# Where VectorE counts slot positions and gates, and where Pool scatters them, beside the latent maxima of a fused attention and expert kernel

## The chip, the cores and the metric

The kernel runs on one core of a Trainium2 chip. What counts is the device time of one execution, in microseconds: the median of three runs is 956.13 (955.96 to 956.14).

## What is computed

Eight batches of 256 tokens with 256 features are normalised. One branch is latent attention (MLA: low-rank queries, keys and values, a rotary part of 64, 16 heads, causal). The other is a transformer block: plain causal attention (MHA, 16 heads), a residual, and a mixture of eight experts of which each token takes two. The output is x + s * silu(f), with s and f the results of the branches. Cut to what bears on the change:

```python
def _moe(x_flat, Wr, Wg, Wu, Wd):
    logits = x_flat @ Wr.T
    top_logits, top_idx = jax.lax.top_k(logits, TOP_K)      # TOP_K = 2, 8 experts
    probs = jax.nn.softmax(top_logits, axis=-1)
    cw = jnp.zeros((T, NUM_EXPERTS), x_flat.dtype)
    cw = cw.at[jnp.arange(T)[:, None], top_idx].add(probs)
    hg = jnp.einsum('eih,th->eti', Wg, x_flat)
    hu = jnp.einsum('eih,th->eti', Wu, x_flat)
    y = jnp.einsum('ehi,eti->eth', Wd, jax.nn.silu(hg) * hu)
    return jnp.einsum('eth,te->th', y, cw)
```

## The kernel before

Each engine has one hand-written queue of instructions; semaphores order them between engines, and nothing reorders them. The attention part is a pipeline over the eight batches b. In each batch TensorE runs four stages: P2 (heads of MHA transposed), T1 (MLA scores of batch b, their exponentials, values, and beside them the MHA scores from which the row maxima are taken), P1 (MLA projections of batch b+1) and T2 (MHA scores of batch b, exponentials and values, and beside them the MLA scores of batch b+1 for their row maxima).

T2 is where the change lies. For each of 16 heads TensorE issues the transposed MHA scores of head h, then the MLA scores of head h-1 of the next batch (`max_head`, into one of two PSUM banks). ACT takes the exponential of head h into `ex`, Pool sets the part above the diagonal to zero (`causal`, an affine_select per head), and for each group of four heads TensorE multiplies by the values (`values`, which waits for the selects of its four heads). VectorE takes the maxima of the MLA scores (`maxima`, two instructions and two reads of an accumulator for each head); TensorE's `max_head(h)` waits for the maxima of head h-2, for its bank. Ahead of the maxima of every second head VectorE rounds two heads of queries (`rounded`, the cast of `qr`), which TensorE waits for too. Behind head 5 TensorE runs `project_v2`, which overwrites the bank ps[1] with the rank counts and so waits for `pst` (the second step of the positions), and behind head 10 `project_qk2`. Both are projections of MHA for the next batch. The stage ends at line L602, where TensorE transposes the row maxima (`max_t`); then P2 starts with transposes that ACT and VectorE (`odd_heads`, the cast of `qt`) move to SBUF.

The routing of batch r = b-1 runs beside this. VectorE finds the top two experts (`top_two`), TensorE counts ranks (`route_ranks`, five small bf16 matmuls in T2 behind head 1), VectorE works out slot positions (`positions`: nine small instructions, most of which wait for one just before) behind the maxima of head 1 and gates (`gates`: four) behind head 4. Pool scatters 4 x 128 slot entries to a list in DRAM by four indirect DMAs (`scatter_slot`), one behind each of the selects of heads 9 to 12. Batch 0's T2 has no routing to do; the T2 of batch 7 has no next batch, so it has no MLA maxima, no projections, and its positions and gates run in one piece; VectorE and ACT split expert weights there instead. After the last T2 the last batch's routing runs alone, and once its slots are scattered the experts' blocks start.

Three functions of VectorE make up what the hooks `after` hold, as `after[h]` runs behind the maxima of head h; `splits` has hooks behind 3, 5, 7, 12 and 14.

## Time and profile before

| | us |
|---|---|
| median of three runs | 956.13 |
| the profiled execution, its time | 958.59 |
| its span, first to last instruction | 956.9 |
| mean granted TensorE clock, share of full | 0.935 |
| TensorE busy | 830.5 (87%) |
| VectorE busy | 625.2 (65%) |
| ACT busy | 501.6 (52%) |
| Pool busy | 392.2 (41%) |

The profile is one execution taken by the hardware profiler. PE is TensorE (PEld its weight loads), DVE VectorE, ACT ScalarE, POOL GpSimd. A line such as L586 is a line of the kernel; helpers that issue many operations have one line for all of them. In brackets stands how long an engine sat idle ahead of an instruction, and which engine's result ended that. The attention part runs to about 652 us; the experts' blocks fill the rest.

### The profile page before, as it was taken

What the parts mean: (1) busy time and instruction counts of PE and PEld (TensorE: products, weight loads), DVE (VectorE), ACT (ScalarE), POOL (GpSimd) and SP (SyncE); (2) the same over time, 40 slices, a digit from 0 to 9 for tenths busy, and PEclk for the clock granted to TensorE, in tenths of its full rate; (3) what the DMA queues carried; (4) which work ended last, traced back from release to release, by engine and by line L of the source; (5) the groups of instructions that cost most, each with busy time, mean ns of one, the idle gap of its engine ahead of it and who ended that gap; (6) DMA issues with size and microseconds to landing.
All of it is one profiled execution on the core that took longest, in us unless ns stands there. A gap on an engine that the chain in (4) does not pass through costs nothing.

```text
span 956.9 us, 18123 instructions
## 1 busy us (share of the span) xinstructions
PE 830.5 (87%) x6432; PEld 743.6 (78%) x6432; DVE 625.2 (65%) x2207; ACT 501.6 (52%) x1089; POOL 392.2 (41%) x538
## 2 busy tenths in 40 slices
PE   5889999999999999999998998965269999998980
PEld 3868978978887887887897897843169999998980
DVE  4876677667677667757758757632257777776754
ACT  3445375366366456456356446540146677776651
POOL 5522432343343334344344344331404756555541
PEclk9878999999999999999999999976579999999995
DMA  8000000000000000000000000030236776889736
GB/s 273 1 1 2 13 1 25 12 2 13 24 1 14 13 13 2 24 12 3 23 13 2 24 12 3 23 144 23 47 134 176 221 220 198 238 240 348 193 53 186
DMA packets 39884, 71.04 MB, mean 74 GB/s; under 512 B 10914, under 2 KB 34850, under 8 KB 36834
## 3 DMA queue, kind: packets, MB, share of 16 engines
q1 hardware_dynamic: 29074, 57.39, 17.6%
q0 software_dynamic: 9856, 12.13, 6.7%
q8 instruction: 52, 0.85, 0.4%
q10 hardware_dynamic: 864, 0.36, 0.2%
q14 instruction: 38, 0.31, 0.1%
HBM read 55.12 MB, written 14.81 MB: 73 GB/s over the span
## 4 chain that ended last, share of the span: by engine, by line
PE 67%; DVE 10%; DMA 9%; issue 6%; POOL 2%; ACT 2%; SPq 2%; POOLq 0%; DVEq 0%; ACTq 0%
PE ps L586 54%; DMA expert_rows<-yo,slot_of 6%; PE ps L679 6%; PE ps L716 3%; DVE ps L1400 2%; PE ps L612 2%; DVE ps L1397 1%; SPq L425 1%; PE ps L621 1%; DVE qr L1237 1%; DMA w_ukv_raw<-in_w_ukv 1%; DMA raw<-in_w_experts 1%; SPq L441 1%; POOL slots L515 1%; POOL expert_rows L563 1%
## 5 line engine op out<-in xcount | busy, mean ns | idle before, releaser
L523 POOL TENSOR_SCALAR_AFFINE_SELECT ex<-ex 128x256 f32<-128x256 f32 x256 | 107.6, 425 | 246.5 <-ACT ex L1101 245.1
L1101 ACT ACTIVATE ex<-ps 128x384 f32<-128x384 f32 x256 | 125.4, 497 | 118.9 <-PE ps L586 116.8
L586 PE MATMUL ps<-qt,kt 128*128 128x256 f32 (+1 forms) x768 | 164.1, 325 | 8.6 <-ACT ex L1101 4.6
L502 POOL TENSOR_TENSOR tok<-tok,swp 128x256 f32<-128x256 f32 x128 | 97.4, 761 | 114.7 <-DVE swp L1362 113.7
L1397 DVE CUSTOM_DVE_ANT_0 ps<-ps,mask 128x128 f32<-128x128 f32 x256 | 77.4, 302 | 94.9 <-PE ps L586 90.5
L586 PEld LDWEIGHTS ps<-qt,kt 128*128 128x128 f32 x768 | 108.9, 193 | 20.7 <-issue 9.8
L563 POOL DMA_INDIRECT expert_rows<-yo,slot_of x46 | 78.5, 1707 | 110.8 <-DMA expert_rows<-yo,slot_of 55.6
L1400 DVE CUSTOM_DVE_ANT_0 ps<-ps,mask 128x256 f32<-128x256 f32 x256 | 118.9, 465 | 0.0
L1241 DVE TENSOR_TENSOR wel<-raw,weh 128x768 fp32r<-128x768 f32 x92 | 88.4, 961 | 37.2 <-ACT weh L971 36.0
L586 PE MATMUL ps<-wh,xth 128*128 128x320 f32 (+2 forms) x352 | 96.9, 358 | 3.7 <-DVE wl L1241 2.8
L1358 DVE TENSOR_TENSOR tok<-ps,cos_t 128x320 f32<-128x320 f32 x128 | 62.9, 491 | 52.8 <-PE ps L586 52.2
L586 PE MATMUL ps<-xeh,weh 128*128 128x256 f32 x368 | 79.4, 298 | 11.8 <-issue 9.9
L971 ACT ACTIVATE qt<-ps 128x512 f32<-128x512 f32 (+1 forms) x96 | 57.2, 596 | 61.9 <-PE ps L679 59.8
L971 ACT ACTIVATE kt<-ps 128x512 f32<-128x512 f32 (+1 forms) x96 | 57.4, 598 | 53.4 <-PE ps L679 48.3
L586 PE MATMUL ps<-wh,xtl 128*128 128x320 f32 (+2 forms) x352 | 84.1, 321 | 0.0
L586 PE MATMUL ps<-wl,xth 128*128 128x320 f32 (+2 forms) x352 | 83.8, 320 | 0.0
L971 ACT ACTIVATE weh<-raw 128x768 fp32r<-128x768 f32 x92 | 77.9, 846 | 10.1 <-DMA raw<-in_w_experts 10.1
L679 PE MATMUL ps<-idf,tok 128*128 128x128 f32 x512 | 77.0, 273 | 0.0
L586 PE MATMUL ps<-xeh,wel 128*128 128x256 f32 x368 | 75.9, 289 | 0.0
L586 PE MATMUL ps<-xel,weh 128*128 128x256 f32 x368 | 75.8, 288 | 0.0
L586 PE MATMUL ps<-kt,qt 128*128 128x128 f32 (+1 forms) x256 | 73.4, 368 | 0.0
L586 PE MATMUL ps<-kr,qr 128*128 128x128 f32 (+1 forms) x256 | 58.6, 316 | 16.8 <-DVE negm L1400 13.1
(160 smaller groups left out, 1918.3 us busy)
## 6 DMA issues: line engine op xcount, KB each, us to landing
raw<-in_w_experts SPq DMA_DIRECT2D x23, 1536.0 KB
mla_branch<-s_b SPq DMA_DIRECT2D x8, 256.0 KB, 2.1
expert_rows<-xn SPq DMA_DIRECT2D x8, 256.0 KB, 2.2
x_normalised<-otk SPq DMA_DIRECT2D x8, 256.0 KB, 2.1
xr<-in_x SPq DMA_DIRECT2D x1, 2048.0 KB
s_tok<-mla_branch SPq DMA_DIRECT2D x1, 2048.0 KB
w_cols_raw<-in_w_cols SPq DMA_DIRECT2D x1, 1792.0 KB, 15.4
x<-expert_rows SPq DMA_DIRECT2D x3, 512.0 KB, 5.2
```

The costliest lines, as they stand in the source:

```text
L502: nc.gpsimd.tensor_tensor(t, t, swp[:, n % 2, :, :], ALU.add).then_inc(tokd, 1)
L523: nc.gpsimd.affine_select(a, a, [[0, 2], [1, P]], ALU.is_ge, zero, 0, -1).then_inc(exm, 1)
L563: nc.gpsimd.indirect_dma_start(ys[:, :], bass.IndirectOffsetOnAxis(mt_b[:, blk, j, 1:2], 0), yo[:, blk % 2, j, :], None, compute_op=ALU.ad ...
L586: return nc.tensor.matmul(o, a, m, start=start, stop=stop, skip_group_check=True, **k)
L679: t = nc.tensor.transpose(ps[2 + n % 2][:, j * P:(j + 1) * P], tok[:, n % 4, j, :], idf[:, :])
L716: i = nc.tensor.transpose(bank2(u)[:, j * P:(j + 1) * P], a[:, p0:p0 + P], idf[:, :])
L971: return nc.scalar.activation(o, a, ACT.Copy)
L1101: nc.scalar.activation(ex[:, h % (2 * G), :], ps[4 + h % 2][:, P:4 * P], ACT.Exp, scale=scale).then_inc(ex_, 1)
L1241: return nc.vector.tensor_tensor(o, a, b.bitcast(F32), ALU.subtract)
L1358: nc.vector.tensor_tensor(tok[:, n % 4, :, 0:HW], a, cos_t[:, tt:tt + 1, :].broadcast_to([P, G, HW]), ALU.mult)
L1397: nc.vector.tensor_tensor_reduce(out=o[:, 0:P], in0=o[:, 0:P], in1=mask2[:, 1, :], scale=-1.0, scalar=-2.0 * BIG, op0=ALU.add, op1=ALU.min ...
L1400: nc.vector.tensor_tensor_reduce(out=o[:, S:2 * S], in0=o[:, S:2 * S], in1=mask2[:, :, :].rearrange("p a k -> p (a k)"), scale=-1.0, scala ...
```

## The change

VectorE's `positions` is divided into five steps and `gates` into three. In the T2 stages of batches 1 to 6 they are no longer two pieces behind the maxima of heads 1 and 4; they go behind the maxima of heads 1, 2, 4, 6, 8 (two steps), 9 and 10. The instructions, their operands and the semaphores that they wait for and raise are as before. Where they run alone (the T2 of batch 7 and behind it) they still follow each other at once. Pool's four scatters of a batch no longer stand between the selects of heads 9 to 13; they stand behind the select of head 15, with one wait for `posd` ahead of the first. This goes for batches 1 to 7.

```diff
@@ block.gpsimd
-            def scatter_slot(r, t, k):
-                if t == 0 and k == 0:
-                    pool.wait_ge(posd, r + 1)
-                nc.gpsimd.indirect_dma_start(slot[:, :], bass.IndirectOffsetOnAxis(posu[:, t, k:k + 1], 0),
-                                             meta[:, t, k, :], None).then_inc(msc, 16)
+            def scatter_slots(r):
+                pool.wait_ge(posd, r + 1)
+                for t in range(2):
+                    for k in range(2):
+                        nc.gpsimd.indirect_dma_start(slot[:, :], bass.IndirectOffsetOnAxis(posu[:, t, k:k + 1], 0),
+                                                     meta[:, t, k, :], None).then_inc(msc, 16)
...
-            def slots_between(r):
-                return {9 + 2 * t + k: lambda t=t, k=k: scatter_slot(r, t, k) for t in range(2) for k in range(2)}
...
                 rope_sums(b + 1)
-                causal(b, ex2, exm2, slots_between(b - 1))
+                causal(b, ex2, exm2, {})
+                scatter_slots(b - 1)
             causal(last, ex1, exm1, {6: lambda: power2(last - 1)})
-            causal(last, ex2, exm2, slots_between(last - 1))
+            causal(last, ex2, exm2, {})
+            scatter_slots(last - 1)
             power2(last)
-            for t in range(2):
-                for k in range(2):
-                    scatter_slot(last, t, k)
+            scatter_slots(last)
@@ block.vector
                     if not first:
-                        after[1] = lambda: positions(b - 1)
-                        after[4] = lambda: gates(b - 1)
+                        in_expert, chosen, summed, kept, stepped = position_steps(b - 1)
+                        plus_one, inverse, both = gate_steps(b - 1)
+                        after |= {1: in_expert, 2: chosen, 4: summed, 6: kept, 8: lambda: (stepped(), plus_one()),
+                                  9: inverse, 10: both}
                     stage_m1(b + 1, after)
...
             def positions(r):
-
-                dve.wait_ge(rnk, r + 1)
...
+                for step in position_steps(r):
+                    step()
 
             def gates(r):
-
-                dve.wait_ge(gex, r + 1)
...
+                for step in gate_steps(r):
+                    step()
```

The steps hold what `positions` and `gates` held, in the same order: `in_expert` pose; `chosen` base and two of posx; `summed` posf; `kept` posu and two of meta (with the wait for the scatters of the batch before); `stepped` rc; `plus_one` and `inverse` gsum; `both` two of meta, which raises `posd`.

## Rows read from the trace of the kernel before

**Rows 1.** The page, the chain that ended last, by engine.

```profile
PE 67%; DVE 10%; DMA 9%; issue 6%; POOL 2%; ACT 2%; SPq 2%; POOLq 0%; DVEq 0%; ACTq 0%
```

**Rows 2.** Timeline of PE at L602: start, us, engine, line, operands, count [idle before <-releaser].

```profile
143.04 0.38 PE L602 MATMUL ps<-idf,negm 128*16 128x128 f32 x2 [0.54 <-DVE negm L1400]
...
219.64 0.39 PE L602 MATMUL ps<-idf,negm 128*16 128x128 f32 x2 [0.34 <-DVE negm L1400]
...
370.21 0.39 PE L602 MATMUL ps<-idf,negm 128*16 128x128 f32 x2 [0.34 <-DVE negm L1400]
...
444.72 0.39 PE L602 MATMUL ps<-idf,negm 128*16 128x128 f32 x2 [0.34 <-DVE negm L1400]
...
595.57 0.39 PE L602 MATMUL ps<-idf,negm 128*16 128x128 f32 x2 [0.34 <-DVE negm L1400]
```

**Rows 3.** Timeline of PE: latent scores of head 0 in batches 0 and 4, head 4.

```profile
126.08 0.49 PE L586 MATMUL ps<-kr,qr 128*128 128x128 f32 x2 [0.21 <-ACT kt L971]
...
425.92 0.50 PE L586 MATMUL ps<-kr,qr 128*128 128x128 f32 x2 [0.21 <-ACT kt L971]
...
430.31 0.47 PE L586 MATMUL ps<-kr,qr 128*128 128x128 f32 x2 [1.12 <-DVE negm L1400]
```

**Rows 4.** Timeline of DVE in T2 of batch 4.

```profile
427.79 0.17 DVE L1521 TENSOR_TENSOR pose<-ps,base 128x16 f32<-128x16 f32 x1
428.00 0.17 DVE L1524 TENSOR_TENSOR base<-ps,base 128x8 f32<-128x8 f32 x1
428.08 0.25 DVE L1526 TENSOR_TENSOR posx<-oh,pose 128x16 f32<-128x16 f32 x2
...
429.10 0.41 DVE L1237 CAST qr<-qt 128x512 fp32r<-128x512 f32 x1
...
431.99 0.16 DVE L1547 TENSOR_SCALAR gsum<-gexp 128x2 f32<-128x2 f32 x1
...
432.66 0.30 DVE L1397 CUSTOM_DVE_ANT_0 ps<-ps,mask 128x128 f32<-128x128 f32 x1
...
440.17 0.76 DVE L1237 CAST qr<-qt 128x512 fp32r<-128x512 f32 x1
```

**Rows 5.** Line L1237 on DVE, 199 to 620 us: ns min/median/max, starts.

```profile
L1237 DVE CAST qr<-qt x46: 412/420/824, 202.1 to 591.0; 128x512 fp32r<-128x512 f32 x46
```

**Rows 6.** Stretches: us, PE busy (x), granted clock, DMA share, GB/s.

```profile
126.00:129.00 3.00, 2.57 (x15) 1.00 0.00 0
...
204.00:206.00 2.00, 2.00 (x12) 0.50 0.00 0
...
580.00:582.00 2.00, 2.00 (x11) 0.50 0.03 8
...
648.00:650.00 2.00, 0.12 (x4) 0.50 0.02 1
```

**Rows 7.** Timelines of ACT, POOL and PE at the end of batch 7's T2.

```profile
645.06 0.93 ACT L1101 ACTIVATE ex<-ps 128x384 f32<-128x384 f32 x2
...
648.69 1.13 POOL L523 TENSOR_SCALAR_AFFINE_SELECT ex<-ex 128x256 f32<-128x256 f32 x3
...
649.88 0.65 PE L586 MATMUL ps<-ex,v 128*32 128x256 f32 x4 [3.02 <-POOL ex L523]
```

**Rows 8.** Timeline of DVE, T2 of batch 0: maxima of heads 5, 10 and 11.

```profile
131.52 0.30 DVE L1397 CUSTOM_DVE_ANT_0 ps<-ps,mask 128x128 f32<-128x128 f32 x1 [0.53 <-PE ps L586]
...
136.76 0.30 DVE L1397 CUSTOM_DVE_ANT_0 ps<-ps,mask 128x128 f32<-128x128 f32 x1 [0.32 <-PE ps L586]
...
138.22 0.30 DVE L1397 CUSTOM_DVE_ANT_0 ps<-ps,mask 128x128 f32<-128x128 f32 x1 [0.71 <-PE ps L586]
```

**Rows 9.** Line L515 on POOL, the scatters: ns min/median/max, starts.

```profile
L515 POOL DMA_INDIRECT slots<-meta,posu x32: 957/977/1220, 211.2 to 675.8; - x32
```

**Rows 10.** Timeline of POOL: first select of batch 7, a scatter behind another.

```profile
601.87 0.41 POOL L523 TENSOR_SCALAR_AFFINE_SELECT ex<-ex 128x256 f32<-128x256 f32 x1 [7.54 <-ACT ex L1101]
...
673.25 0.96 POOL L515 DMA_INDIRECT slots<-meta,posu  x1 [0.30 <-issue]
```

More of the change, by code:

```diff
@@ L1543, in gates, with position_steps, in_expert, chosen @@
-            def gates(r):
-                dve.wait_ge(gex, r + 1)
-                g = meta[:, :, :, 2].bitcast(F32)
-                nc.vector.tensor_scalar(gsum[:, :], gexp[:, :], 1.0, None, ALU.add).then_inc(gst, 1)
-                dve.wait_ge(gst, 3 * r + 2)
-                nc.vector.reciprocal(gsum[:, :], gsum[:, :]).then_inc(gst, 1)
-                dve.wait_ge(gst, 3 * r + 3)
-                copy(g[:, :, 0], gsum[:, :])
-                nc.vector.tensor_tensor(g[:, :, 1], gexp[:, :], gsum[:, :], ALU.mult).then_inc(posd, 1)
+            def position_steps(r):
+                def in_expert():
+                    dve.wait_ge(rnk, r + 1)
+                    nc.vector.tensor_tensor(pose[:, :, :], ps[1][:, 0:2 * NE].rearrange("p (t e) -> p t e", t=2),
+                                            base[:, :].unsqueeze(1).broadcast_to([P, 2, NE]), ALU.add).then_inc(pst, 1)
+                def chosen():
+                    dve.wait_ge(pst, 6 * r + 2)
+                    nc.vector.tensor_tensor(base[:, :], ps[1][:, 2 * NE:3 * NE], base[:, :], ALU.add).then_inc(pst, 1)
+                    for t in range(2):
+                        i = nc.vector.tensor_tensor(posx[:, t, :, :], oh[:, t, :, :],
+                                                    pose[:, t:t + 1, :].broadcast_to([P, 2, NE]), ALU.mult)
+                    i.then_inc(pst, 1)
+                def summed():
+                    dve.wait_ge(pst, 6 * r + 4)
+                    nc.vector.tensor_reduce(posf[:, :, :].rearrange("p t k -> p (t k)"),
+                                            posx[:, :, :, :].rearrange("p t k e -> p (t k) e"), AX.X,
+                                            ALU.add).then_inc(pst, 1)
+                def kept():
+                    dve.wait_ge(pst, 6 * r + 5)
+                    wait(dve, msc, 64 * r)
+                    copy(posu[:, :, :], posf[:, :, :])
+                    ids = rc[:, C_IDS:C_IDS + 8].rearrange("p (t k f) -> p t k f", t=2, k=2)
+                    for t in range(2):
+                        i = copy(meta[:, t, :, 0:2], ids[:, t, :, :])
+                    i.then_inc(pst, 1)
+                def stepped():
+                    dve.wait_ge(pst, 6 * r + 6)
+                    step = rc[:, C_IDS:C_IDS + 8].rearrange("p (a f) -> p a f", f=2)
+                    nc.vector.tensor_scalar(step[:, :, :], step[:, :, :], 2.0 * P, None, ALU.add).then_inc(gst, 1)
+                return in_expert, chosen, summed, kept, stepped
@@ new lines, in gate_steps, with plus_one, inverse, both @@
+            def gate_steps(r):
+                g = meta[:, :, :, 2].bitcast(F32)
+                def plus_one():
+                    dve.wait_ge(gex, r + 1)
+                    nc.vector.tensor_scalar(gsum[:, :], gexp[:, :], 1.0, None, ALU.add).then_inc(gst, 1)
+                def inverse():
+                    dve.wait_ge(gst, 3 * r + 2)
+                    nc.vector.reciprocal(gsum[:, :], gsum[:, :]).then_inc(gst, 1)
+                def both():
+                    dve.wait_ge(gst, 3 * r + 3)
+                    copy(g[:, :, 0], gsum[:, :])
+                    nc.vector.tensor_tensor(g[:, :, 1], gexp[:, :], gsum[:, :], ALU.mult).then_inc(posd, 1)
+                return plus_one, inverse, both
```

21 lines of the change are left out of this document (removed).

## The prediction, as it was put on record

> **What bounds the kernel now.** I read the chain of work that ended last first: TensorE holds two thirds of it, VectorE a tenth, Pool 2% [rows 1]. So the question is not which engine is busiest but where TensorE waits inside the stages that the change touches. The second view is the timeline of TensorE at line L602, which moves a batch's row maxima for the latent branch and so closes stage T2. From that of batch 0 to that of batch 6 there are six periods in 452.53 us [rows 2], the first and the last line of it. The period of batch 4 is 444.72 - 370.21 = 74.51, that of batch 1 is 219.64 - 143.04 = 76.60. T2 itself runs from the score matmul of the first latent head to L602: 425.92 to 444.72 = 18.80 in batch 4 [rows 2, 3], so the other stages of a period take 74.51 - 18.80 = 55.71. I take that as the same in each batch; the six T2 stages with positions then sum to 452.53 - 6 x 55.71 = 118.3, of which batch 1 has 20.9.
>
> Batch 0 is the comparison that the kernel carries itself. Its T2 has no positions, no gates and no scatters, and takes 143.04 - 126.08 = **16.96** [rows 2, 3]. Batch 4 takes 1.84 more. What lies between shows in three places. (a) TensorE stands 1.12 before head 4's latent scores at 430.31, released by negm, which VectorE writes in its maxima [rows 3]. In that time VectorE ran the positions: 427.79 to 429.10 = 1.31, in one piece between maxima 1 and 2 [rows 4]. (b) The gates, 431.99 to 432.66 = 0.67 [rows 4], cost nothing now: TensorE runs the projection project_v2 just then, and head 5's scores would not be there earlier. (c) The cast of qr at 440.17 takes 0.76 [rows 4], against a median of 0.42 of 46 such casts [rows 5]; a scatter of Pool runs beside it.
>
> A third view, the stretches with their granted clock, adds a cost that the busy times hide. [...]
>
> Last, the T2 of batch 7. It has no latent maxima beside it, so Pool is what ends last. ACT ends the last two exponentials at 645.06 + 0.93 = 645.99; Pool's selects of heads 13 to 15 start only at 648.69, behind the fourth scatter, and TensorE stands 3.02 for them until 649.88 [rows 7]. All that follows (heads to tokens, output, router, last scatters) hangs on that chain.
>
> **The change, part by part.** *Positions and gates in pieces (six stages, batches 1 to 6).* The same 13 instructions stay. In one piece a dependent one starts 0.21 after the one before (427.79 to 428.00), an independent one 0.08 (428.00 to 428.08) [rows 4]. With maxima between them the results are there long before, so I price each at 0.08: 13 x 0.08 = 1.04 instead of 1.31 + 0.67 = 1.98. Where each lands, against the slack that VectorE has in batch 0:
> - behind maxima 1, pose: 0.08 to 0.21, ahead of maxima 2, which TensorE's wait (a) hangs on. Counted 0.1.
> - behind 2 and 4: base, two posx (0.24) and the sum (0.08): VectorE waits 0.53 before maxima 5 in batch 0 [rows 8]; covered. If project_v2 were not there, 0.3 would be paid.
> - behind 6: posu and two copies to meta, 0.24 by pitch, up to 0.5 where they meet a select of Pool. Maxima 7 follow at once in the trace, and TensorE's score 9 waits for them. On the path: 0.24.
> - behind 8 and 9: three instructions, 0.24 to 0.4 against 0.32 of slack before maxima 10 [rows 8]: 0 to 0.1, taken 0.05.
> - behind 10: two, 0.16 against 0.71 before maxima 11 [rows 8]: covered by project_qk2 on TensorE.
> - new waits: each is on VectorE's own earlier step, on gex (done at about head 3) or on the scatters of the batch before (70 us old). project_v2 waits for base, which now ends before head 4's scores do: nothing.
> - the rank matmuls, which batch 0 lacks: 0.1 on TensorE.
>
> *Pool's scatters behind select 15.* A scatter takes 0.957 to 1.220, median 0.977, in 32 [rows 9]; back to back one starts about 1.26 after the other (0.96 and 0.30 of issue) [rows 10]. Four are 5.0. In the middle stages they leave the selects of heads 10 to 15 free; that was no bound there (values of the last group follow the maxima), but cast (c) loses its neighbour: its excess of 0.34 goes. In exchange the scatters now lie beside VectorE's last cast of ks: 0 to 0.34, taken about half, 0.15. Queued behind the scatters on Pool are the selects of the next stage: the first of them comes at 601.87 in batch 7 [rows 10], 6.3 behind L602 (595.57 [rows 2]), and Pool's idle before it is 7.54; that is the room for 5.0, with what select 15 comes earlier on top. Behind the scatters of batch 6, in batch 7, stands power2(7), which waits for the chain heads to tokens, output and residual, longer than 5.0: covered.
>
> The new T2 by this: 16.96 + 0.1 + 0.24 + 0.05 + 0.1 + 0.15 = **17.6**. Six of them are 105.6 instead of 118.3: **12.7 less**. This holds a clock that no longer falls, which is 4.7 of the 12.7 (batches 1, 3 and 6 above their equals: 1.7 + 1.5 + 1.5). I take it so because batch 0, with the wait gone, keeps 1.00 throughout.
>
> *The last T2.* Without scatters, select 15 starts at 645.99 + 0.06 and ends 0.41 later: 646.5 instead of 649.8, and the last values start about 646.5 instead of 649.88: **3.4 less**. Bounds: 2.6 if the last two selects meet VectorE's split of expert weights and take twice their 0.4; 5.0 if TensorE's clock, at half from 648 on [rows 6] after the long wait, then stays up for the last values and the transposes behind them.
>
> [...]
>
> **Rivals.**
> 1. *The clock still falls* in about three of six stages. For it: batch 4 has the wait too (1.12 [rows 3]) and no fall, so something else has a part in it. Against: batch 0. It gives 16.1 - 4.7 = 11.4 less: 944.7.
> 2. *VectorE pays every piece.* If slack I call cover is used up (VectorE is the engine whose maxima the scores wait for), T2 is 16.96 + 1.04 + 0.1 + 0.15 = 18.25 and six save 8.8; with 3.4 this is 12.2: 943.9, and with rival 1 948.6.
> 3. *Slower: four scatters stop VectorE at a stage boundary.* Just behind L602 VectorE's casts of qt are links of the chain that opens the next stage, and three or four scatters now fall there. If each of four stops VectorE for its whole 0.98, a period gains 3.9, six 23.5, against 16.1 saved: 963.5. It decides from 16.1 / 6 = 2.7 per period. Against: the casts of qt read PSUM, and VectorE's PSUM maxima keep their length under today's scatters; only SBUF casts stretch.
> 4. *Nothing changes*: 956, if ACT's exponentials, not VectorE, set the pace of the stage. The wait of 3.02 in batch 7 speaks against it alone, and batch 0, where the same exponentials fit into 16.96.
>
> **How the numbers follow.** The sum is made against the profiled execution: span 956.9, its time 958.6, the median of the runs 956.13, so 2.5 lower. I subtract 12.7 + 3.4 = 16.1 from the median: **940.0**; should the timed runs lack one of the three clock falls, it is 1.5 more. Chances: forecast 0.57 (937 to 942.5), rival 1 0.17, rival 2 0.19 (both together within it), rivals 3 and 4 and the unnamed 0.07. Low end: T2 at 17.3 (1.8 more saved) and 5.0 in the last: 936.6. High end: rival 1 or 2 with one more us lost: 946.5. A measurement of this kernel can tell 0.2% (1.9 us) from no change: faster 0.93, same 0.03, slower 0.04.
>
> **What would show it.** In the new trace: periods at L602 near 73.3, all six alike; no wait over 0.3 before score 4; clock 1.00 through T2; casts of qr at 0.42 for head 12; in batch 7 the last values released within 0.7 of the last exponential. Wrong if TensorE's waits for negm move to score 9 with more than 0.5, if VectorE's casts of qt get longer, or if the first select of the next stage waits for nothing but Pool itself.

## The result, and the profile after

| | before | after |
|---|---|---|
| median, us | 956.13 (955.96 to 958.5) | 934.21 (932.99 to 935.59) |
| ratio | | 0.9766, 95% interval 0.9743 to 0.9788 |
| profiled execution, its time | 958.59 | 935.21 |
| its span | 956.9 | 933.3 |
| mean granted TensorE clock | 0.935 | 0.948 |

The change saves 21.9 us, 2.3%. The forecast was 940.0, so 16.1 saved, and its range ended at 936.6: the direction was right, the size was not, and the result lies below the range. Which chip these runs had is not on record. In two later sets, on chips 3 and 6, the same kernel had ratios of 0.978 and of 0.991. The second of these is a finding of its own, told under the experiments.

The chain of work that ended last in the kernel after. TensorE's share was 67% [rows 1].

```profile
PE 71%; DMA 8%; DVE 8%; issue 5%; ACT 4%; POOL 2%; SPq 0%; POOLq 0%; ACTq 0%; DVEq 0%
```

The timeline of TensorE at the line that closes T2, now L600 (it answers to [rows 2]; start, us, engine, line, operands, count, in brackets the wait before):

```profile
143.13 0.38 PE L600 MATMUL ps<-idf,negm 128*16 128x128 f32 x2 [0.54 <-DVE negm L1398]
...
216.12 0.39 PE L600 MATMUL ps<-idf,negm 128*16 128x128 f32 x2 [0.45 <-DVE negm L1398]
...
362.86 0.39 PE L600 MATMUL ps<-idf,negm 128*16 128x128 f32 x2 [0.45 <-DVE negm L1398]
...
435.87 0.39 PE L600 MATMUL ps<-idf,negm 128*16 128x128 f32 x2 [0.45 <-DVE negm L1398]
...
581.90 0.39 PE L600 MATMUL ps<-idf,negm 128*16 128x128 f32 x2 [0.45 <-DVE negm L1398]
```

Six periods take 581.90 - 143.13 = 438.77 instead of 452.53: 13.76 less. Batch 4's is 73.01 instead of 74.51, batch 1's 72.99 instead of 76.60; one of the six has 73.74 (0.7 more, between the end of T2 and that of the next T1, in this execution alone), the others 72.99 to 73.02.

TensorE in T2 of batch 4, the latent scores of heads 0 and 4 (they answer to [rows 3]):

```profile
418.56 0.50 PE L584 MATMUL ps<-kr,qr 128*128 128x128 f32 x2 [0.21 <-ACT kt L969]
...
421.92 0.47 PE L584 MATMUL ps<-kr,qr 128*128 128x128 f32 x2
```

The stage takes 435.87 - 418.56 = 17.31 (18.80 before), and head 4's score waits for nothing, where it stood 1.12. VectorE in the same stage (it answers to [rows 4]):

```profile
420.43 0.17 DVE L1522 TENSOR_TENSOR pose<-ps,base 128x16 f32<-128x16 f32 x1
...
426.18 0.16 DVE L1235 CAST posu<-posf 128x4 uint32<-128x4 f32 x1
426.25 0.23 DVE L1235 CAST meta<-rc 128x4 uint32<-128x4 f32 x2
426.39 0.29 DVE L1395 CUSTOM_DVE_ANT_0 ps<-ps,mask 128x128 f32<-128x128 f32 x1
...
430.28 0.17 DVE L1235 COPY meta<-gsum 128x2 f32<-128x2 f32 x1
430.36 0.16 DVE L1568 TENSOR_TENSOR meta<-gexp,gsum 128x2 f32<-128x2 f32 x1
431.14 0.30 DVE L1395 CUSTOM_DVE_ANT_0 ps<-ps,mask 128x128 f32<-128x128 f32 x1 [0.63 <-PE ps L584]
431.74 0.42 DVE L1235 CAST qr<-qt 128x512 fp32r<-128x512 f32 x1
```

The pieces stand between maxima. The one behind head 6 costs 426.39 - 426.18 = 0.21; behind the last piece VectorE still waits 0.63 for TensorE, so those pieces are covered. The cast of head 12's queries is back at 0.42.

The end of batch 7's T2 and what hangs on it (it answers to [rows 7]), and the clock there (stretch, length, TensorE's busy time and instructions, granted clock, DMA share, GB/s; it answers to [rows 6]):

```profile
632.14 1.53 POOL L524 TENSOR_SCALAR_AFFINE_SELECT ex<-ex 128x256 f32<-128x256 f32 x3 [0.48 <-ACT ex L1099]
632.22 0.93 ACT L1099 ACTIVATE ex<-ps 128x384 f32<-128x384 f32 x2
...
633.72 0.86 PE L584 MATMUL ps<-ex,v 128*32 128x256 f32 x16 [0.31 <-POOL ex L524]
...
638.76 1.99 PE L584 MATMUL ps<-wo,otf 128*128 128x256 f32 x8 [0.69 <-ACT otf L969]
```

```profile
204.00:206.00 2.00, 2.00 (x26) 1.00 0.00 0
580.00:582.00 2.00, 1.55 (x31) 1.00 0.05 9
...
634.00:638.00 4.00, 2.25 (x28) 1.00 0.02 1
638.00:642.00 4.00, 2.07 (x9) 1.00 0.04 5
```

The wait for the selects is 0.31 instead of 3.02, and in this execution TensorE's clock stays full to 642. Before, it was at half there and beyond, and the output projection took 3.78. That row stood outside what I had shown; here it is, from the kernel before, with its clock:

```profile
656.91 3.78 PE L586 MATMUL ps<-wo,otf 128*128 128x256 f32 x8 [0.69 <-ACT otf L971]
```

```profile
650.00:654.00 4.00, 3.35 (x24) 0.50 0.00 0
654.00:658.00 4.00, 2.21 (x7) 0.50 0.00 0
```

The 1.99 of the projection does not come with every execution of the changed kernel. In the profile of the second set below, the same stretch of work runs at full clock up to the projection (1.00 from 626 to 638) and at half in it (0.50 from 639 to 642):

```profile
638.03 3.17 PE L584 MATMUL ps<-wo,otf 128*128 128x256 f32 x8 [0.69 <-ACT otf L969]
```

Over all profiles without the long wait for the selects the projection takes 1.99 to 3.78, with it 3.40 to 3.78. What does recur, in the profiles of the second and third set, is the stretch from the last values to the projection's start: 7.04 with the wait, 5.05 without.

**Where the 23.6 us between the two profiled spans went.** Six periods: 13.76. From the max_t of batch 7's T1 to the last values: 2.48 (27.41 to 24.93). From the last values to the output projection's start: 1.99 (649.88 to 656.91 = 7.03; 633.72 to 638.76 = 5.04), and with the projection itself up to the residual 3.77. From there to the first expert matmul 0.3. In the experts 3.4 (267.17 to 263.76), of which more below. The rest, under 0.1, is the start of the first period.

### The profile page after: what moved, and what is told of

The parts are those of the page before. It is cut to its first block, busy times and chain, and to the rows that moved or that the text cites. A ratio compares the mean times of both kernels' runs of the same rounds, so it can differ in the third digit from the quotient of the medians.

```text
span 933.3 us, 18123 instructions
## 1 busy us (share of the span) xinstructions
PE 823.7 (88%) x6432; PEld 738.2 (79%) x6432; DVE 618.8 (66%) x2207; ACT 500.8 (54%) x1089; POOL 390.8 (42%) x538
## 4 chain that ended last, share of the span: by engine, by line
PE 71%; DMA 8%; DVE 8%; issue 5%; ACT 4%; POOL 2%; SPq 0%; POOLq 0%; ACTq 0%; DVEq 0%
PE ps L584 57%; PE ps L677 6%; DMA expert_rows<-yo,slot_of 5%; PE ps L714 3%; DVE ps L1398 2%; PE ps L610 2%; ACT ex L1099 2%; DVE ps L1395 1%; DMA xg<-x_normalised,slot_of 1%; PE ps L909 1%; PE ps L619 1%; DMA w_ukv_raw<-in_w_ukv 1%; DMA raw<-in_w_experts 1%; POOL expert_rows L561 1%; DVE xr L1686 1%
## 5 line engine op out<-in xcount | busy, mean ns | idle before, releaser
L1186 ACT ACTIVATE sg<-ps 128x256 f32<-128x256 f32 x92 | 35.7, 388 | 70.9 <-PE ps L584 70.9
```

The source lines that it names most:

```text
L1186: nc.scalar.activation(sg[:, n % 2, :], ps[n % 3][:, 0:BS], ACT.Silu).then_inc(sgd, 1)
```

## The experiments

Five sets of kernels ran, each with the kernel before beside it on the same chip; ratios are to that. The first set ran on chip 12, the second and the third on chip 3, the fourth on chip 6 and the fifth on chip 5. Two kernels of the first set ran again on chip 3 and are told here with it.

**First set: one part at a time.** The changed kernel with the scatters back between the selects:

```diff
-                causal(b, ex2, exm2, {})
-                scatter_slots(b - 1)
+                causal(b, ex2, exm2, slots_between(b - 1))
```

> VectorE's positions and gates in pieces as in the changed kernel; Pool's four scatters stay between the selects of heads 9 to 13. Theory A (the two edits need each other): posd now comes behind the maxima of head 10, so Pool stands behind select 9 with the selects of heads 10 to 15 queued behind it; four scatters of 1.0 and six selects from there put the last select some 2.5 us behind its place in the changed kernel. T2 of batches 1 to 6 about 19.8 us against 17.3, last T2 as before: near 957 us. Theory B (the edits add up): T2 about 17.6, time near 944.

Measured: 978.24, ratio 1.0182 (1.0131 to 1.0233), slower than the kernel before. Theory A has the mechanism, as the rows below show, but not its price: T2 took 20.2 to 20.9 and not 19.8, and the clock behind it was not counted. I ran it again on another chip, to see whether it was the program's:

> The changed kernel with the scatters of batches 1 to 7 back between selects 9 to 13 (the same program as the first run of this kind, ratio 1.0182 on another chip). Theory A (split in pieces, the position numbers are ready only after head 9, so Pool stands at its first scatter and the selects 12 to 15 queue behind four scatters at the stage's end; it is the program's): periods of 76.6 to 78.5 us again, the clock at half at the end of each T2, ratio 1.014 to 1.022. Theory D (it was that chip's): ratio 0.98 to 1.00.

Measured: 971.97, ratio 1.0187 (1.0162 to 1.0213), periods of 76.55 to 78.52. It is the program's. The timeline of Pool and TensorE at the end of its T2 of batch 4, and the clock there:

```profile
442.60 1.03 POOL L522 DMA_INDIRECT slots<-meta,posu  x1 [2.73 <-DVE meta L1575]
...
448.55 1.12 POOL L533 TENSOR_SCALAR_AFFINE_SELECT ex<-ex 128x256 f32<-128x256 f32 x3
...
449.72 1.51 PE L591 MATMUL ps<-ex,v 128*32 128x256 f32 x16 [2.58 <-POOL ex L533]
```

```profile
450.00:454.00 4.00, 4.00 (x30) 0.50 0.02 4
```

Split in pieces, the gates are ready only behind head 10. Pool, whose first scatter stands behind select 9, waits 2.73 for them with six selects queued behind, and the last values stand 2.58. The granted clock is 0.50 for 3.4 us at the end of T2 in batch 2 and for 6.8 us in the five others, and in all six P2 starts at half. The two parts of the change are not independent: the split is worth something only once the scatters have left the selects.

The other part alone, kernel before plus the scatters behind select 15 (batches 1 to 7):

```diff
-                causal(b, ex2, exm2, slots_between(b - 1))
+                causal(b, ex2, exm2, {})
+                scatter_slots(b - 1)
```

> The kernel before, with Pool's scatters of batches 0 to 6 behind select 15 of the next batch's T2. Theory A: the middle T2 stages lose only the long cast of qr (0.3 each, some 2 us), the wait for the positions and the falls of the clock stay; the last T2 loses its wait of 3.0 and TensorE keeps its full clock behind it (2.5 + 3.8): 948 us. Theory B (most of the gain is Pool's): near 940.

Measured: 970.54, ratio 1.0109 (1.0072 to 1.0145): 1% slower where 948 was expected, a miss. Again on another chip:

> The kernel before with the four scatters of batches 1 to 7 behind the stage's last select, positions and gates left whole (the same program as the run of this kind before it). There ScalarE's last eviction of the values and all of P2 behind it came some 2.4 us late in each of six batches though every engine but Pool runs the program of before. If that is the program's (theory C), the same waits of 2.6 us show again and the ratio is 1.01. If it came from that chip or hour (theory D), the waits are absent, each period is that of the kernel before or a little less, and the ratio is 0.985 to 0.995 from the last T2 alone.

Measured there: 948.95, ratio 0.9933 (0.9888 to 0.9978). Only Pool's program differs from the kernel before, and it was slower on chip 12 and faster on chip 3. I come back to this in the last two sets.

Two more: the scatters of batch 7 alone moved; and, in the kernel before, 24 transposes of the unit matrix ahead of the last values, to keep TensorE at work through its wait for Pool:

```diff
+                    closing[15] = lambda: [mm(ps[3][:, 0:P], idf[:, :], idf[:, :], True, True) for _ in range(24)]
```

> The kernel before, with only the scatters in batch 7's T2 moved behind select 15. Theory A: 2.5 us of wait and 3.8 us of TensorE at half clock behind it go: 949.8 us, and the six periods at the row maxima stay as they were. Theory B (the clock behind the last values does not hang on that wait): 3 us less, 953.

> The kernel before, with 24 matmuls of 128 columns into an unused PSUM bank ahead of the last group's values of batch 7; they run in the wait for Pool and their result is used by nothing. Theory A: the last values still start 3 us late, but the clock stays at full and what follows to the residual takes 7.1 us instead of 10.9: 952.3 us. Theory B (the chain behind the values was shortened by something other than the clock): 956 us, unchanged.

Measured: the first 953.10, ratio 0.9912 (0.9878 to 0.9946), some 8 less where 6.3 were expected; the interval has room for both. Its projection took 3.78 although the wait was gone. The second 957.13, ratio 0.997 (0.9948 to 0.9992), some 3 less where 4 were expected. TensorE and Pool in it (24 transposes are 48 instructions):

```profile
644.54 5.62 PE L586 MATMUL ps<-idf 128*128 128x128 f32 x48
646.43 1.13 POOL L523 TENSOR_SCALAR_AFFINE_SELECT ex<-ex 128x256 f32<-128x256 f32 x3
650.09 0.86 PE L586 MATMUL ps<-ex,v 128*32 128x256 f32 x16
```

The selects are done at 647.56, but the transposes run until 650.16, so the last values start some 2.5 behind the selects. The clock holds (1.00 from 636 to 655), and the stretch from the last values to the output projection is 5.05 instead of 7.03, as in the changed kernel. So about 2 of the 3.77 behind the last values are the clock alone and need no earlier select. The projection fell to half clock all the same (0.50 from 655.6 on; it took 3.44). From the last max_t to the router's matmuls it is 44.75, no less than the 43.4 to 44.8 of the kernels with the wait: in its profile the transposes cost what the clock gave back, and the 3 us of its median can't be put down to the last T2.

**Second set: undo the last T2, and the experts' start.** The changed kernel with two selects on a scratch tile behind each of selects 9 to 12 of batch 7, 3.3 us of Pool in the place of the scatters; batches 1 to 6 untouched. The changed kernel ran beside it.

> The changed kernel itself again, beside the other three of this set, so that they are compared with it on one chip. Theory A (the split of positions and gates takes the stalls out of T2, the moved scatters take the select wait out of the last T2): ratio 0.977 to the kernel before, 21 to 22 us less, and in its trace no wait of ScalarE for its last values' eviction (ov) in batches 1 to 6. Theory C (what held ScalarE back at the stage's end in the kernel with the moved scatters alone, 2.6 us each in all six batches, belongs to the scatters behind select 15 wherever they stand): the same wait shows here, and the ratio is nearer to 0.99.

> The changed kernel, with two selects on a scratch tile behind each of selects 9 to 12 of batch 7 (some 0.41 us each, 3.3 us in all), in the place where the scatters stood. Theory A (the last T2's gain is Pool reaching its last selects earlier, and that wait lets TensorE's clock fall): the select wait ahead of the last values is back at some 3 us, the clock is at half for the projection behind it, and the time is 5 to 7 us above the changed kernel. Theory B (the last T2's gain came from positions and gates split, Pool's place is cover): at most 3 us above it.

Measured: 935.21 for the changed kernel, ratio 0.9778 (0.9737 to 0.982), and 942.40, ratio 0.9864 (0.9825 to 0.9903), with the delay: 7.2 more. Its timeline:

```profile
636.19 1.51 PE L596 MATMUL ps<-ex,v 128*32 128x256 f32 x16 [2.24 <-POOL ex L527]
...
643.22 3.78 PE L596 MATMUL ps<-wo,otf 128*128 128x256 f32 x8 [0.69 <-ACT otf L981]
```

```profile
634.00:638.00 4.00, 1.51 (x16) 0.58 0.01 0
638.00:642.00 4.00, 2.55 (x11) 0.50 0.03 2
```

The wait is back, the clock falls ahead of the projection, which takes 3.78 against 3.17 in the changed kernel beside it. From the last max_t to the router's matmuls it is 44.3 against 38.5 in the changed kernel beside it: 5.8, of which 3.2 lie ahead of the last values and 2.6 behind them. That shows Pool's place in batch 7 as the cause of the last T2's gain. Its size between two profiles varies with the projection: 6.25 in those of the result, 5.8 here, 4.5 on chip 6 (43.4 against 38.9).

The experts' start: SyncE loads 23 slot lists before it asks for the third block's weights. I moved the fifteen whose address comes from a register behind that load:

```diff
             for blk in range(2, NB):
                 sp.wait_ge(weld, 4 * (blk - 1))
                 if blk < NSTAT:
                     load(blk, w_experts[blk, :, :])
+                    if blk == 2:
+                        for j in range(NDYN):
+                            row = sp.value_load(bmap[0:1, 1, j:j + 1], min_val=0, max_val=SLOTS - BS)
+                            load_slots(NSTAT + j, slot[bass.ds(row, BS), :])
```

> The changed kernel, with the fifteen slot lists whose addresses are read from a register moved on SyncE's queue from ahead of the third block's weights to behind them. Theory A (how long that run of slot lists holds the queue, 21.9 us in the changed kernel's trace and 24.4 before, decides when the third block's weights are asked for, and that is the 3.4 us at the start of the experts and the two levels 2.4 us apart): the weights are asked for as soon as VectorE is done with the first block, ScalarE's wait for them falls from 5.8 us to under 2, all executions are of one level at or under 933 us on the first chip (ratio 0.973 or less). Theory B (the levels come from elsewhere): the two levels stay and the median is that of the changed kernel.

Measured: 927.90, ratio 0.9704 (0.9667 to 0.974). SyncE in the changed kernel, then here:

```profile
660.10 21.88 SPq L425 DMA_DIRECT2D slot_of<-slots  x23
682.02 16.24 SPq L422 DMA_DIRECT2D raw<-in_w_experts  x3
```

```profile
659.94 3.96 SPq L425 DMA_DIRECT2D slot_of<-slots  x8
664.44 0.36 SPq L422 DMA_DIRECT2D raw<-in_w_experts  x1
665.86 16.39 SPq L425 DMA_DIRECT2D slot_of<-slots  x15
```

The weights are asked for 4.5 us after the first list instead of 21.9, ScalarE's wait of 5.75 for them (6.65 in the changed kernel beside it) is gone, and from the first expert matmul to the end it is 257.1 instead of 264.0: the queue is worth 7 us, and this is a faster kernel than either of the two.

**Third set: what T2 is bound by.** On top of that kernel (once more as the base), the step `kept` (posu and two of meta) moved from behind head 6 to behind head 10, and `stepped` with it from behind head 8:

```diff
-                        after |= {1: in_expert, 2: chosen, 4: summed, 6: kept, 8: lambda: (stepped(), plus_one()),
-                                  9: inverse, 10: both}
+                        after |= {1: in_expert, 2: chosen, 4: summed, 8: plus_one, 9: inverse,
+                                  10: lambda: (kept(), both(), stepped())}
```

> The changed kernel with the fifteen register-addressed slot lists behind the third block's weights, once more, as the base for the next one. On the chip before it had a ratio of 0.9704 and four executions from 926.8 to 928.4 us. If the gain is the queue's, the ratio is 0.970 here too, and the stretch from the first expert matmul to the end is 257 us (264 in the changed kernel).

> The kernel with the slot lists behind the load, and VectorE's copy of the gates behind head 6 (kept) moved behind head 10, where it goes with the last two pieces: nothing of it stands between heads 6 and 8 any more. Theory A (T2 is bound by VectorE from its first maximum on, so that each instruction on it counts, 0.21 us for this one): the periods of batches 1 to 6 fall from 73.01 to 72.8, 1.2 to 1.4 us less in all, 0.998 of its base. Theory B (from head 9 on TensorE and the exponentials bound T2, and VectorE has 0.2 us to spare): the periods stay 73.01 and the time is that of its base.

Measured: the base 928.15, ratio 0.9728 (0.9705 to 0.975); with the step late 926.94, ratio 0.9716 (0.9696 to 0.9735), the fastest kernel here, though the two intervals overlap. In the traces the periods fall from 73.01 to 72.87 (437.36 against 438.36 over six). So 0.14 of the 0.21 was on the path: theory A, somewhat smaller.

The kernel before with eight transposes of the unit matrix ahead of score 4, in T2 of batches 1 to 6:

```diff
+                        if h == 5 and max_head in warm:
+                            for _ in range(8):
+                                mm(ps[6][:, 0:P], idf[:, :], idf[:, :], True, True)
```

> The kernel before with eight transposes of the unit matrix (into a bank that is free there) ahead of latent score 4 in T2 of batches 1 to 6, where TensorE waits for the maxima behind the block of positions and gates. Theory A (the stall itself lets TensorE's clock fall, in some batches of most executions, and a fall costs 1.5 to 1.8 us): no stretch of batches 1 to 6 shows a clock under 1.00, each period is 74.9 us (as in the profile of the kernel before that had no fall), 449.4 from the first to the seventh against 452.5 in the profile of before, and the median is 2 to 4 us under before's. Theory B (the falls come from elsewhere): as many falls as before, median unchanged.

Measured: 949.12, ratio 0.9942 (0.992 to 0.9964), 5.5 to 6 us less; expected were 2 to 4. TensorE's clock in its T2 stages, the first, the fourth and the last looked at:

```profile
204.00:206.00 2.00, 2.00 (x20) 1.00 0.00 0
...
426.00:430.00 4.00, 4.00 (x37) 1.00 0.00 0
...
580.00:582.00 2.00, 1.91 (x16) 1.00 0.03 8
```

No fall in any of the six (1.00 from 79 to 621), and periods of 74.52 to 74.84, 447.47 in all, while VectorE's block of positions is where it was. That shows the wait at score 4 as the cause of the falls. It isn't sufficient for one: the profile of the 24 transposes above, with the wait in place, has no fall in batches 1 to 6 either (449.4), and the kernel before on a further chip had one large one (periods of 74.51 to 76.31, 450.24). Nor does its length decide: in one program and one trace the wait is either 1.11 to 1.12 or 1.48 to 1.49, and in the profile of before batch 1 fell behind 1.49, batches 3 and 6 behind 1.11, and batch 5 did not behind 1.48. A fall costs 1.5 to 1.8 per period where the clock is down for 3 to 4 us. In one profile of the fourth set (the kernel before with the slot lists late) two of four falls last between 6 and 7 us and cost 2.8 each.

With these the periods come apart, by stretches from T1's max_t to T2's in batches without a fall, at equal waits at score 4. Where the wait is 1.12: 46.40 before, 45.74 with the scatters moved. Where it is 1.48: 46.76 and 46.16. With both parts of the change 44.90, with `kept` late 44.75. So the scatters' place is worth 0.6 to 0.7, the split 0.84 or 1.26 by which wait it takes away, and the falls the rest.

**Fourth set: is the experts' gain the change's?** Both kernels with a profile on one chip, and two variants of the kernel before: the slot lists behind the load, and scatters moved plus the eight transposes.

> The kernel before itself with a profile, beside the changed kernel on one chip. In the profiles so far the stretch from the first expert matmul to the end is 3.4 us longer before than after, and SyncE's run of slot lists ahead of the third block's weights takes 24.4 us before and 21.9 after; but four kernels of one chip all had 24.4 and six of another all 21.9. Theory C (the longer run belongs to the chip or the execution): here it is the same for both kernels of this set, and the stretch of the experts differs by under 1 us. Theory A (the change shortens it): 24.4 here and 21.9 in the changed kernel.

> The changed kernel on the same chip. Theory C: the run of slot lists as long as in the kernel before beside it, the experts' stretch within 1 us of it, and the difference of the two spans is the six periods (13 to 14 us, less if the kernel before has no fall of TensorE's clock in T2 here) and the last T2 with its projection (6 to 7 us), 19 to 21 us. Theory A: 23 us with 3 of them in the experts.

> The kernel before with the fifteen register-addressed slot lists behind the third block's weights. If this run of loads bounds the experts' start whatever stands ahead of it, the gain is that of the changed kernel's version: 7 to 8 us, ratio 0.992. If it was cover in the kernel before (its weights late for another reason), under 3 us.

> The kernel before with the scatters of batches 1 to 7 behind the last select and eight transposes of the unit matrix ahead of score 4 in T2 of batches 1 to 6, positions and gates left in one block: all that the change brings but the split itself. Theory A (the split's own worth is the 1.5 us wait at score 4, of which VectorE wins back all but 0.8 us by the end of T2, and the clock): periods of 73.8 us without a fall, 442.8 from the first to the seventh against 438.2 in the changed kernel, ratio 0.983 to 0.986. Theory B (the wait itself costs nothing once the clock is held): 438 to 440, ratio 0.98 or less.

Measured: kernel before against itself 1.0025 (0.9987 to 1.0063). Changed kernel 951.47, ratio **0.9912** (0.9876 to 0.9947), where the two sets before had 0.977 and 0.978. Slot lists 949.54, ratio 0.9885 (0.9841 to 0.9928), some 10 less (7 to 8 expected; runs scatter more on this chip: 952.99 to 963.37 in 21 of the kernel before, against 952.73 to 957.08 in 8 in the third set), and 256.8 from the first expert matmul to the end against 266.8: the queue bounds that start in the kernel before as well. The last one 955.99, ratio 0.9953 (0.9928 to 0.9977), not the 0.985 expected. The run of slot lists took 24.4 to 24.5 in both profiled kernels (theory C), and from the first expert matmul to the end it was 266.8 before and 264.8 after. In ten other profiles the run is 21.9 on chip 3 and 24.1 to 24.9 on chips 6 and 12, whatever the kernel. The profile of before has 24.4 and that of after 21.9, so these two may well come from different chips. The stretch itself varies as much without a cause in the program: with the experts' part unchanged it is 261.4 to 265.4 in five profiles on chip 3 and 264.7 to 268.4 in four on chip 12. So no run shows that the 3.4 is the change's.

But the time of the changed kernel needs a reason. Its T2 stages are as short as in the result (44.89 to 44.94 for the stretch), yet from T2's max_t to T1's it takes 29.9 to 30.5 instead of 28.1, behind batches 1 to 5, and 28.7 instead of 26.9 behind batch 6: 9.8 + 1.8 us in all. Behind batch 0, which has no scatters, it is 28.1. The timeline of ScalarE, Pool, TensorE and VectorE there, batch 4:

```profile
439.91 0.86 PE L584 MATMUL ps<-ex,v 128*32 128x256 f32 x16
439.96 0.38 ACT L969 ACTIVATE ov<-ps 128x256 f32<-128x256 f32 x1 [1.23 <-PE ps L584]
...
440.72 0.96 POOL L516 DMA_INDIRECT slots<-meta,posu  x1 [0.30 <-issue]
441.44 0.60 PE L714 MATMUL ps<-idf,qs 128*128 128x128 f32 x4
441.98 0.96 POOL L516 DMA_INDIRECT slots<-meta,posu  x1 [0.30 <-issue]
442.88 0.38 ACT L969 ACTIVATE ov<-ps 128x256 f32<-128x256 f32 x1 [2.54 <-remote]
443.25 0.95 POOL L516 DMA_INDIRECT slots<-meta,posu  x1 [0.30 <-issue]
...
444.38 0.69 DVE L1235 CAST qt<-ps 64x512 fp32r<-64x512 f32 x1 [3.22 <-issue]
```

The last values end at 439.91 + 0.86 = 440.77; ScalarE's eviction of them starts 2.11 later. The transposes at 441.44 end at 442.04; VectorE's cast of them starts 2.34 later. Ends of matmuls are modelled in a profile, but by these ScalarE and VectorE take up TensorE's results some 2 us late while the four scatters run one behind the other. In the profile of the result the same two instructions follow at once (in batch 4 ScalarE's eviction at 435.50, behind values that end at 434.57 + 0.86 = 435.43; VectorE's cast at 436.80, behind transposes that end at 436.10 + 0.60 = 436.70). The wait shows in the profiles of four kernels, all with four scatters behind the last select, on three chips (12, 6 and 5), and in none of the kernels with scatters between selects on the same chips. It is also what made the second kernel of the first set slow: there the stretch from T2's max_t to T1's is 1.9 to 3.2 longer. The fourth kernel of this set has it too (1.8 to 3.2 a stage, 15.1 in all against 11.6 in the changed kernel), more than its miss of the 0.985. Its stretch from T1's max_t to T2's, 46.17 to 46.19 against 44.89 to 44.94, puts the split alone at 1.26 on this chip. The kernel before with the same eight transposes had 46.40 in five of its six stages, so between these two the scatters' place is worth only 0.2: the parts do not simply add.

**Fifth set: take the scatters apart.** Base: changed kernel with the slot lists behind the load. Against it the same, with the scatters of batches 0 to 5 one by one in the following T1, where Pool waits 1.6 to 2.2 for the next exponential:

```diff
+            def apart(r):
+                one = [lambda t=t, k=k: scatter_slot(r, t, k) for t in range(2) for k in range(2)]
+                return {3: one[0], 6: lambda: (one[1](), power2(r + 1)), 11: one[2], 14: one[3]}
...
-                causal(b, ex1, exm1, {6: lambda: power2(b - 1)})
+                causal(b, ex1, exm1, apart(b - 2) if b > 1 else {6: lambda: power2(b - 1)})
                 rope_sums(b + 1)
                 causal(b, ex2, exm2, {})
-                scatter_slots(b - 1)
```

> The changed kernel with the fifteen slot lists behind the third block's weights, as the base on this chip. On two chips (the third of these sets and the one before it) the scatters behind the last select cost nothing; on the two others ScalarE and VectorE stood 2 to 3 us at the start of P2 while the four scatters ran one behind the other, in each of six batches. If this chip is of the first kind: ratio 0.971, periods of 73.0 us, no such wait. If it is of the second kind: periods of 74.8 to 75.4 us with ScalarE's wait of 2.6 us at its last eviction of the values, and a ratio of 0.982 to 0.986.

> The same, with the scatters of batches 0 to 5 taken apart: each stands alone behind select 3, 6, 11 or 14 of T1 of the following batch, where Pool waits 1.6 to 2.2 us for the next exponential. Theory E (four scatters one behind the other, 0.3 us apart, beside P2 are what holds ScalarE and VectorE back on some chips): on a chip of either kind the periods are 72.9 to 73.3 us and no wait of 2.6 us shows; on one of the second kind the ratio to its base is 0.986 to 0.99, on one of the first kind 1.00. Theory F (any scatter beside TensorE's signals costs there): on a chip of the second kind the waits move into T1, the exponentials behind selects 3, 6, 11 and 14 come late, and the period stays over 74.5 us.

Measured: the base 941.38, ratio 0.9846 (0.9815 to 0.9878), with ScalarE's waits of 2.5 to 2.6 in six batches; so this chip is of the second kind. Taken apart: **930.49**, ratio 0.9727 (0.9696 to 0.9757), 0.988 of its base. All six periods are 73.00 to 73.03 (74.8 to 76.1 in the base from the second on). The start of P2, and a scatter alone:

```profile
434.32 0.38 ACT L977 ACTIVATE ov<-ps 128x256 f32<-128x256 f32 x1 [0.83 <-PE ps L592]
...
435.62 0.69 DVE L1243 CAST qt<-ps 64x512 fp32r<-64x512 f32 x1 [0.98 <-PE ps L722]
...
444.39 0.99 POOL L516 DMA_INDIRECT slots<-meta,posu  x1 [0.16 <-issue]
446.45 0.40 POOL L533 TENSOR_SCALAR_AFFINE_SELECT ex<-ex 128x256 f32<-128x256 f32 x1 [1.07 <-ACT ex L1107]
```

Theory E holds: single scatters hold nobody back, on a chip where four in a row do, and each fits into a wait that Pool had. Whether the row as such or its place beside P2 does the harm, this run can't say, since it changed both.

## Why the prediction was wrong, step by step

- **The periods** (predicted 12.7 less, measured 13.76). Right in mechanism: no wait at score 4, clock full, T2 of 17.31 in batch 4 where 17.6 was predicted, the rest of the period 55.70 where 55.71 was assumed. The copy behind head 6 cost 0.21 (0.24 predicted), the pieces behind heads 8 and 9 and the cast of ks (0.29 at 434.48, not stretched) nothing, where 0.2 were charged. The division was off in part: I gave the scatters' place 0.34 - 0.15 = 0.2 per period and it is worth 0.6 to 0.7; the split, which I gave 1.1, is worth 0.84 in the four stages with the shorter wait and 1.26 in the two with the longer.
- **The clock in T2** (4.7 of the 12.7). In the trace of before the granted clock is 0.50 for some 3.4 us in T2 of batches 1, 3 and 6, from 204.0, 354.2 and 579.4 on, and 1.00 in the T2 of the others. From T1's max_t to T2's these three take 48.50, 47.91 and 47.84 where batches with an equal wait and no fall take 46.76, 46.40 and 46.40: 1.74 + 1.51 + 1.44 = 4.7. Right: in three profiles of the changed kernel the stretch from T1's max_t to T2's is 44.88 to 44.95 in every batch, so no T2 has a fall, and dummy work at the same wait removes them in the kernel before. Rival 1 is out. That the kernel before had three falls and not one or none is luck of its profile; its other profile has one.
- **The last T2** (predicted 3.4, bounds 2.6 to 5.0; measured 2.48 + 3.77 = 6.25). This is the step that failed. The term priced the wait for the selects, which went nearly as predicted (3.02 to 0.31, the last values 2.48 earlier), and put the clock behind it at nothing in the sum and at 1.6 in the bound, for the last values and the transposes behind them. Those alone gave 1.99 (7.03 to 5.04). I left out the output projection, eight matmuls that take 3.78 at half clock and 1.99 at full, 1.79 more. The trace of before had both: the clock of 0.50 in [rows 6, last line] and the 3.78. Bringing Pool's delay back cost 7.2 in the median. The 1.99 recurs in every pair of profiles on chip 3; the projection's 1.79 came in full in the profile of the result, and only 0.6 of it in the changed kernel's next one (3.17). Why the clock falls there in some executions and not in others, behind the same waits, is open.
- **Behind the attention part** (predicted nothing). About 1.9 of the medians' 21.9 are in neither term. Between the profiles 3.4 lie in the experts, no more than that stretch varies between kernels whose experts are the same; the cause is open.
- **Rival 2**, VectorE pays every piece, is out: T2 is 17.31 and not 18.25, and VectorE waits 0.63 behind the last piece. It holds for the one piece that I had on the path, of which 0.14 were paid.
- **Rival 3**, four scatters at the stage boundary, came true on three of the four chips that the record names (12, 6 and 5, not 3), at its place and with the instruction named (VectorE's cast of qt, and ScalarE's eviction beside it), but not as four stops of 0.98: each engine starts once some 2 us late, and the cast itself takes its usual 0.69. In the changed kernel on chip 6 it cost 1.8 to 2.4 a stage, under the 2.7 that was the point of decision, so the change stays faster there, at 0.991; on chip 5, in the version with the lists late, 1.8 to 3.1. I had given it a part of 0.07, on the ground that the casts read PSUM. The profile of the result doesn't show it.
- **The cast of ks beside a scatter** (priced at 0 to 0.34, taken 0.15; measured nothing). Beside the first scatter of batch 4 it took 0.29, its usual time. Yet other casts do wait for a scatter's end. The cast of 440.17 ends at 440.93; beside it stands this scatter in the trace of before, which ends at 440.71:

```profile
439.73 0.98 POOL L515 DMA_INDIRECT slots<-meta,posu  x1 [0.17 <-issue]
```

Eleven of the twelve casts of qr that overlap a scatter there end 0.22 to 0.23 behind its end, whatever their start. In both profiles of the kernel with the split alone the last casts of ks take 0.74 to 0.77 instead of 0.28 and end 0.09 behind the scatter's end. What decides is when the cast starts. Beside scatters of 0.97 to 0.98, casts that start up to 0.24 in keep their time and those that start 0.3 to 0.5 in wait for the end. Beside the first scatter of a batch, of 1.03, a cast that starts 0.46 in still keeps its time, and one that starts 0.7 in waits. The ks of the changed kernel, at 0.45 into the first one, is of the kind that keeps it. This holds for casts of qr and ks. The casts of qt, from `ps`, keep their 0.69 beside a scatter wherever they start (0.16 to 0.86 in, over all profiles). Why the start decides is not shown.
- The high end of the range, 946.5, doesn't follow from its sentence, which gives 944.7 + 1.0 = 945.7. Nothing hangs on it.

With the measured 6.25 in the term of the last T2 the forecast would have been 937.2, still 3.0 above the 934.21. With the projection's 1.79 in the bound alone the low end would have been 934.8, 0.6 above it.

## What to carry to other kernels

When a wait on the critical path goes, look up TensorE's granted clock behind it, and price everything that runs at half clock until it recovers, not only the waiting instruction; as a range, since the clock may fall there for another wait. Dummy work that is to hold the clock has to end with the wait: here 24 transposes outlasted it by 2.5 us. Two edits that feed one queue are priced together: here the split alone cost 1.8 to 1.9%; the move alone gained 0.7% or cost 1.1% and both gained 2.2 to 2.3% or 0.9%, by the chip. And a row of scatters on Pool is better set one by one into waits that Pool has anyway: on a chip where the row costs, it was 1.2% faster.

## What the runs showed of the hardware

- One program has ratios of 0.977, 0.978 and 0.991 to the same other program in three sets, the last two on chips 3 and 6, with interval half widths of 0.2 to 0.4%. Two marks went together on chips 12 and 6: ScalarE's and VectorE's waits of 2.5 to 4 us beside four scatters in a row, and 24.1 to 24.9 us instead of 21.9 for the same 23 list loads of SyncE. Chip 5 has the waits too. That it is the chip and not the hour is likely, as the two sets on chip 3 agree (0.970 and 0.973 for one program); on none of the three chips with the waits did a second set run.
- Beside four scatters 0.30 apart, ScalarE and VectorE took up TensorE's finished work 2.1 and 2.3 us late on such a chip (batch 4); beside a scatter with a select or a wait behind it they did not (on chip 5, from T2's max_t to T1's 28.13 us with the scatters apart, 29.9 to 31.3 with four in a row). By which road is open, and matmul ends are modelled; TensorE's own next instructions, released by VectorE, start on time (L714 at 441.44).
- TensorE's granted clock fell from 1.00 to 0.50 behind a wait of 1.1 to 1.5 us in some batches and executions and not in others, in one program; keeping it at work over the wait with transposes whose result nobody reads saved 5.5 to 6 us over six T2 stages.
- A scatter held casts of qr and ks to its own end: casts of 0.42 us ended 0.22 to 0.23 behind it, casts of 0.28 us 0.09 behind it. It did so only to casts that started some way in: none at 0.24 or less into a scatter of 0.97 to 0.98, all between 0.3 and 0.5. Casts of qt, from `ps`, kept their 0.69 us.
